# Splitting the sixteen output transposes of the graph stage around one tile's scores

## The reference, cut to what matters

```python
def _forward(v, q, adj, ...):                 # B=8, N=512, F=512, H=16, 20 keys
    self_feat = concat(v, q_exp) @ W_self.T + b_self
    output = self_feat
    for d in range(2):                        # two directions
        cond, vb = A.sum(-1), A @ w_bias + b_bias
        output = output + _gat_attention(self_feat, cond, vb, ...)
    return v + relu(output)
# _gat_attention: aff = q.k / sqrt(dh); masked and biased by label; softmax over 20 keys;
#                 weighted sum of 20 key rows; projection per head
# then, in the second layer: ln = (h - mu) / sqrt(var + eps); h = gamma * ln + beta; ...
```

## Time and profile before

| | |
|---|---|
| median of 3 runs | 1300.29 us (1295.09 to 1304.65) |
| the profiled execution | 1299.49 us, its span 1297.7 us |
| mean granted TensorE clock | 0.972 of full speed |
| TensorE busy | 1217.1 us, 94% of the span |
| VectorE, GpSimd busy | 885.7 us and 886.2 us, 68% each |
| graph stage, steps 1 to 7 | from about 122 us to about 429 us of the span |
| one step of it | 44.0 us |

### The profile page before, as it was taken

One profiled execution on the slowest core, in us unless ns is written; L12 is line 12 of the kernel. 1 busy time (PEld: TensorE's weight loads), 2 busy tenths in 40 slices (PEclk: granted clock), 3 DMA queues, 4 the chain that ended last, 5 costly groups with the idle time before them and its releaser, 6 DMA issues.

```text
span 1297.7 us, 18236 instructions
## 1 busy us (share of the span) xinstructions
PE 1217.1 (94%) x6040; PEld 830.8 (64%) x6040; DVE 885.7 (68%) x1443; ACT 632.7 (49%) x1104; POOL 886.2 (68%) x565
## 2 busy tenths in 40 slices
PE   6989999999999879899999999999899999999984
PEld 4447777777777666566666666676566666666642
DVE  2454778878877766657766676676676677677755
ACT  1323453456355535455465465465465465465551
POOL 1115477776776846676796787788698788788834
PEclk9979999999999889999999899999899999999998
DMA  9884255536444564423534533533524534534411
GB/s 331 325 295 151 41 210 222 182 130 236 172 171 157 184 202 142 117 64 107 146 73 111 141 88 108 147 86 105 145 78 111 149 80 113 147 85 111 115 38 57
DMA packets 106525, 184.01 MB, mean 142 GB/s; under 512 B 38864, under 2 KB 50448, under 8 KB 101184
## 3 DMA queue, kind: packets, MB, share of 16 engines
q1 hardware_dynamic: 99216, 167.24, 42.3%
q10 hardware_dynamic: 7216, 15.62, 4.0%
HBM read 83.92 MB, written 48.01 MB: 102 GB/s over the span
## 4 chain that ended last, share of the span: by engine, by line
PE 54%; DMA 3%; DVE 3%; SPq 1%; issue 1%; ACT 0%; POOL 0%; ACTq 0%; DVEq 0%; POOLq 0%
PE a_bank L1795 10%; PE a_bank L107 8%; PE a_bank L1808 8%; PE a_bank L108 8%; PE a_bank L109 8%; PE a_bank L1844 8%; DMA sk_stack<-kl 3%; PE a_bank L1855 2%; SPq L1310 1%; DVE keep L1660 1%; DVE rden L1678 1%; PE a_bank L1838 1%; PE a_bank L1819 1%; DMA sq_stack<-sht 0%; ACT pt L1557 0%
## 5 line engine op out<-in xcount | busy, mean ns | idle before, releaser
L1660 DVE TENSOR_REDUCE keep<-a_bank 128x1 f32<-128x512 f32 x496 | 333.7, 674 | 219.3 <-PE a_bank L1808 217.9
L1557 ACT ACTIVATE pt<-a_bank 128x512 f32<-128x512 f32 x512 | 303.5, 597 | 363.5 <-PE a_bank L1795 355.8
L1408 POOL TENSOR_TENSOR acc<-acc,pt 128x1024 f32<-128x1024 f32 x120 | 286.6, 2388 | 14.8 <-ACT pt L1557 4.1
L1795 PE MATMUL a_bank<-sq_stack,sk_stack 98*128 98x512 f32 x512 | 220.2, 430 | 13.7 <-issue 11.3
L1808 PE MATMUL a_bank<-sk_stack,sq_stack 96*128 96x512 f32 x496 | 202.2, 408 | 7.6 <-DMA sk_stack<-kl 5.1
L1403 POOL TENSOR_TENSOR acc<-pt 128x1024 f32<-128x1024 f32 x60 | 143.4, 2391 | 58.3 <-PE a_bank L1855 43.8
L1795 PEld LDWEIGHTS a_bank<-sq_stack,sk_stack 98*128 98x128 f32 x512 | 98.2, 192 | 104.0 <-issue 70.9
L1086 PE MATMUL g_bank<-m,sf 128*128 128x320 f32 x512 | 140.3, 432 | 1.5 <-ACT g_bank L770 1.5
L1678 DVE RECIPROCAL rden<-a_bank 128x128 f32<-128x128 f32 x128 | 120.4, 943 | 19.5 <-PE a_bank L1838 19.5
L1844 PE MATMUL a_bank<-pt,v 128*32 128x512 f32 x1024 | 123.0, 598 | 0.0
L1086 PEld LDWEIGHTS g_bank<-m,sf 128*128 128x128 f32 x512 | 96.6, 190 | 40.7 <-issue 1.9
(11 more groups left out here) (200 smaller groups left out, 2413.9 us busy)
## 6 DMA issues: line engine op xcount, KB each, us to landing
sq_stack<-qh SPq DMA_DIRECT2D x256, 64.0 KB, 2.0
sk_stack<-kh SPq DMA_DIRECT2D x256, 64.0 KB, 2.0
m<-m_rows SPq DMA_DIRECT2D x8, 1600.0 KB, 6.5
xraw<-in_x_t SPq DMA_DIRECT2D x8, 1024.0 KB, 8.7
xn<-in_x SPq DMA_DIRECT2D x8, 1024.0 KB, 5.3
t_rows<-houth SPq DMA_DIRECT2D x8, 1024.0 KB, 3.9
t_rows<-houtl SPq DMA_DIRECT2D x8, 1024.0 KB, 6.5
hh<-t_rows SPq DMA_DIRECT2D x16, 512.0 KB, 4.1
```

Source lines behind the costliest of these rows:

```text
L1408: nc.gpsimd.tensor_tensor(acc[:, two, :], acc[:, two, :], pt[:, step + 1, two, :], ALU.add).then_inc(s["sum_done"], 1)
L1557: nc.scalar.activation(pt[:, i, 2 * half + k, :], bank[:, k, :], ACT.Exp).then_inc(s["exp_done"], 1)
L1660: nc.vector.reduce_max(mx[:, half, k, n:n + 1], bank[:, 2 + e % 2, :], AX).then_inc(s["emax_done"], 1)
L1795: nc.tensor.matmul(bank[:, k, :], sk[c % 2][0:3 * DH + 2, j, i * P:(i + 1) * P], sq[c % 2][0:3 * DH + 2, j, :], start=True, stop=True).the ...
```

## The change

The transposes of batch b-1 are issued in two halves, with the scores of tile 1 of batch b between them. `back` gets a range of tiles. Its two waits at the head (L1124, L1125) are now issued twice. No instruction of another engine is changed, and no transfer.

```diff
-            def back(b):
+            def back(b, first=0, end=NT):
                 pe.wait_ge(s["att_done"], 4 * b + 4)
                 pe.wait_ge(s["wl_done"], TILES * b + TILES)
-                for i in range(NT):
+                for i in range(first, end):
                     if i >= 2:
                         pe.wait_ge(s["h_done"], 4 * b + i - 1)
                     for f in range(FC):
...
                 scores(b, par, 0, 1)
-                back(b - 1)
-                scores(b, par, 1, NT)
+                back(b - 1, 0, 2)
+                scores(b, par, 1, 2)
+                back(b - 1, 2, NT)
+                scores(b, par, 2, NT)
```

## The result

| | before | changed |
|---|---|---|
| median (4 runs each) | 1297.69 us (1294.82 to 1304.65) | 1324.42 us (1314.12 to 1327.9) |
| ratio | | 1.020, 95% interval 1.0158 to 1.0242 |
| profiled execution, span | 1299.49, 1297.7 us | 1326.15, 1324.3 us |
| one step, mean of six | 44.02 us | 47.79 us |
| mean granted TensorE clock | 0.972 | 0.963 |

The forecast was 1327 us, for the profiled execution 1326 us. Both landed within 3 us, which is less than the executions of one kernel differ among themselves (10 us before, 14 us changed).

The account below looks back on a forecast made before the run. TensorE was taken as the bound, busy 42.77 of 44.00 us a step. The profiled span of 1297.7 us plus 18.0 us of waits and 8.5 us of clock gave 1324.2 us, hence a median of 1327 us, range 1311 to 1341.

Parts of the forecast that it names:

- The stall that goes: TensorE's transposes: the wait for VectorE's residual addition and a short second stop go, gaining 1.05 us a step.
- The second half comes 3.40 us late: TensorE's transposes of tiles 2 and 3 start 3.40 us later, moving VectorE's and ScalarE's chain by as much.
- The cover is 0.74 us, the net price 2.43 us: Scores of tile 3 wait for ScalarE's bias: 3.40 us late, 0.74 us hidden, 2.43 us a step lost after VectorE's saving.
- The saving at L986: VectorE's variance addition, moved past GpSimd's addition, should take 0.17 us instead of 0.40 us.
- The last step, 3.4 us: In the seventh step the end of the softmax counts, so the whole 3.4 us reaches the path.
- The clock, 1.7 us in five steps of six: Behind the wait before tile 3's scores TensorE falls to 1.2 GHz for 3.3 us: 8.5 us in all.
- the case of the held clock: Rival: the waits come but TensorE's clock does not fall behind them; 1318 us, chance 0.24.
- The three terms of the sum: Waits of 14.6 us in six steps and 3.4 us in the last, and 8.5 us of slower clock.
- The split that gains what it shows: Rival: tile 1's scores fill the stall and no bias is late; 1293 us, chance 0.05.
- The mostly hidden wait: Rival: slack hides most of the new wait, a step loses below 1 us, clock stays; about 1305 us, chance 0.07.
- The longer fall of the clock: Rival: the slower clock behind the wait costs 3.0 us in each of six steps; 1336 us, chance 0.08.

Follow-up runs that it names:

- the kernel with the split around half of tile 0: Kernel before, with transposes in halves around the second direction of tile 0's scores and ScalarE's store moved behind its first attention-weights copy: 1289.5 us, ratio 0.9957.
- half a tile: Changed kernel with only one direction of tile 1's scores between the transpose halves, the other behind them: 1302.0 us, ratio 1.0063.
- two tiles: Changed kernel with the scores of tiles 1 and 2 between the transpose halves instead of tile 1 alone: 1363.7 us, one run.
- the kernel with the read moved: Changed kernel with VectorE's read of tile 1's scores between its additions and ScalarE's tile 3 bias ahead of its first normalisation, in six of seven steps: 1318.0 us.
- the filler kernel: Changed kernel plus six matmuls, into a bank nobody reads then, between the scores of tiles 2 and 3: 1311.3 us, ratio 1.0135.
- the unsplit kernel: Kernel before, with the scores of tile 1 ahead of all sixteen transposes, which are not split: 1330.4 us, one run.

## Why the prediction was right

**The stall that goes.** I had 1.05 us a step. The stall left all seven steps, and the kernel with the split around half of tile 0 realises it: 44.02 less 43.10 is 0.92 us.

**The second half comes 3.40 us late.** From the first transposes to the second it was 1.78 us before, now 5.18 us: 3.40 us. Tiles moved by half or twice as much (half, two tiles) give tile 3 at 11.45, 13.60 and 17.90 us behind the first transposes, with the second half at 3.03, 5.18 and 9.49 us: the slope is one.

**The cover is 0.74 us, the net price 2.43 us.** It was 2.28 us, by the start of tile 3. VectorE's additions started 0.64 us behind the transposes, not 0.69, and TensorE 0.74 us behind ScalarE's bias, not 0.85, which makes the cover 0.85 us: 0.05 + 0.11 = 0.16 us. The saving at L986 came as said, 0.17 us in the changed kernel, with GpSimd's addition over before it. The kernel with the read moved shows from the other side, with 1.49 us for `nmr`, that it is the meeting with GpSimd that costs. The Trainium skill (SBUF — State Buffer, Who interferes with whom) says that a VectorE instruction with two inputs in SBUF contends with a GpSimd instruction that reads SBUF, and that the port pair which the two share is an exclusive lock. The row of `nmr`, which has two inputs in SBUF, agrees: it ends 0.02 us behind GpSimd's. L986 has one tensor input, so this sentence does not reach it, but its row behaves alike. In the kernel before it ended at 244.89, and GpSimd's row is this one, ending at 244.87:

```profile
243.32 1.55 POOL L659 TENSOR_TENSOR e<-e,cadd 128x640 f32<-128x640 f32 x1
```

In the last kernel of the experiments, where the chain runs earlier, L986's instruction meets more of that addition and takes 1.07 us (241.07 to 242.14, GpSimd's addition ending at 242.10).

**The last step, 3.4 us.** From its first transposes to the first attention transposes behind the stage's loop it was 26.60 us and is 30.00 us. I had also said that some tenths could come from VectorE's reader of tile 3. It did wait, 0.54 us. But the kernel with the read moved, whose last step has the same order and the same wait of 3.07 us without a fall behind it, took 29.91 us for the same stretch: the fall is worth about 0.1 us there.

**The clock, 1.7 us in five steps of six.** It was 3.77 - 2.28 = 1.49 us in all six. Two small errors, one in each direction, met: 8.5 us forecast, 8.9 measured. The filler kernel isolates it: the same wait with the array at work, and no fall. That it came six times out of six is the property of this one order, in whose steps wait and fall lie alike, and no rule: with the read moved, waits as long were followed by a fall in five steps of six and by none in the seventh. So the number of falls could not be had from the rows that I used, and to come within 0.4 us on it was in part luck. A single execution among the four of the changed kernel, at 1314.12 us, had a mean clock of 0.972 instead of 0.961 to 0.963. It lies near the 1318 us that I gave the case of the held clock. But the kernel before, in its 29 runs beside the last experiments, went from 1289 to 1306 us, its mean clock from 0.979 to 0.968, so the difference can as well lie outside this stage; no trace decides it.

**What luck added.** The three terms of the sum came to 13.7 + 3.4 + 8.9 = 26.0 us where I had 26.5. The span grew by 26.6 us, because four differences that stood in no term (-1.0, +0.3, +1.9 and -0.5 us, from the account of the span above) come to +0.6 us together. Each term is right within 1 us by its own measurement; that the total is right to 0.1 us is luck.

**What I had missed**, without harm to the sum: the second cover at ScalarE's store, worth 0.35 us a step and hidden behind the slowed clock here; and 1.9 us between the last transposes of the stage and the first scores of the next. That stretch took 28.8 us before and 27.9 to 32.6 us in the other traces. In the changed kernel 0.5 us of the 1.9 lie ahead of the second half of these transposes, where VectorE waits for the reload of `x`; most of the rest lies where the clock reads 0.50 for 3.4 us from 492.9, and read 1.00 at the same place before. What sets its length was not tested.

**The rivals.** The split that gains what it shows needed 3.40 us of cover and had 0.85; it holds only where the second half isn't moved back, and there by 5.7 us instead of my 7.3. The mostly hidden wait is what half a tile gives. The longer fall of the clock came with the longer wait (two tiles), in three steps of the unsplit kernel and in two of the kernel with the read moved, not here.

## What to carry to other kernels

A stall on the bounding engine is filled well only by work that doesn't move back what it was about to release. Before splitting a block, follow its second half through the other engines' queues to where the first engine meets it again, and compare the shift with the cover there: 4.3 us of useful work put into a 0.74 us stall cost 2.3 us. And price a new wait on TensorE twice, once as time and once for the matmuls behind it, which here ran at half the clock; and take the second price as a range, since waits of the same length did not all cost it.

## What the runs showed of the hardware

- TensorE, idle for 3.07 us between dense matmuls, was granted 1.2 GHz behind it in seven steps of seven of the changed kernel, and behind 2.9 us in seven of seven of the unsplit one. With the read moved it fell behind five of six waits of 2.9 to 3.0 us, and not behind one of 3.07 us. Idle for 0.92 us (half a tile) it stayed at 2.4 GHz in seven of seven.
- Where the fall starts is not tied to the end of the wait: 0.3 us before it in the changed kernel, from 0.9 us before to 1.5 us behind it in the other two.
- Six matmuls whose result nobody reads, in the 3.07 us, held the clock in seven of seven steps and gained 1.1 us a step.
- With waits of 2.9 to 3.1 us the slowed stretches were 3.4 or 6.8 us long. With waits of 7.4 us they were 6.8 or 10.2 us long, of which 3.2 to 4.6 us still lay in the wait.
- A small VectorE instruction can lose many times its own length beside GpSimd: 0.16 us became 1.49 us on a tensor of 128x4, and 0.17 us became 0.40 and 1.07 us on one of 128x3, each ending within 0.04 us of the end of a GpSimd addition of 128x640.
